# Deformable stage: ScalarE's queue issues seven of the fifteen position loads of a band

## The reference, cut to what matters

```python
offsets = conv2d(x, offset_w, offset_b)              # 18 channels: 9 taps, y and x
mod = jax.nn.sigmoid(conv2d(x, mod_w, mod_b))
sy = base_y[None, None, :, None] + off[:, 0]
sx = base_x[None, None, None, :] + off[:, 1]
...
sampled = (1.0 - wy1f) * ((1.0 - wx1f) * g00 + wx1f * g01) + wy1f * ((1.0 - wx1f) * g10 + wx1f * g11)
out = jnp.einsum('bckp,ock->bop', sampled, wk).reshape(B, O, Ho, Wo)
out = out * mod.mean(axis=1, keepdims=True) + bias[None, :, None, None]
```

## Time and profile before

| what | value |
|---|---|
| median of 3 runs | 3482.6 us (3479.66 to 3482.98) |
| the profiled execution, its time | 3484.76 us |
| its span, first to last instruction | 3483.1 us |
| mean granted TensorE clock | 0.861 of full |
| PE busy, share of the span | 2587.9 us, 74% |
| DVE busy | 2105.3 us, 60% |
| ACT busy | 1818.8 us, 52% |
| POOL busy | 1148.6 us, 33% |

### The profile page before, as it was taken

How to read it: one execution, slowest core, us unless ns; L and a number is a source line. 1 busy time by engine, 2 the same in 40 slices (tenths; PEclk the granted TensorE clock), 3 DMA queues, 4 the chain that set the end, 5 groups by cost and what they waited for, 6 DMA issues and landing times. The chain is left out here.

```text
span 3483.1 us, 86393 instructions
## 1 busy us (share of the span) xinstructions
PE 2587.9 (74%) x38569; PEld 1522.5 (44%) x38569; DVE 2105.3 (60%) x2867; ACT 1818.8 (52%) x1855; POOL 1148.6 (33%) x788
## 2 busy tenths in 40 slices
PE   1773838375999809599999927499993468999998
PEld 1763313124777603255555512277772124555554
DVE  5996766844555466366666566355554645666664
ACT  1211735663555538366656647355553655665565
POOL 0220000104555317444444310155541364334441
PEclk7886969687999959699999968699997787999999
DMA  2455030411111172122222250111115321222221
GB/s 59 129 152 155 1 97 16 177 18 26 33 26 31 37 279 42 47 73 75 75 70 73 70 207 7 27 27 27 30 30 195 122 52 59 72 72 73 72 71 54
DMA packets 213124, 257.74 MB, mean 74 GB/s; under 512 B 79188, under 2 KB 141192, under 8 KB 210696
## 3 DMA queue, kind: packets, MB, share of 16 engines
q1 hardware_dynamic: 203528, 218.58, 21.9%
q0 software_dynamic: 9216, 33.56, 2.4%
HBM read 153.52 MB, written 98.57 MB: 72 GB/s over the span
## 5 line engine op out<-in xcount | busy, mean ns | idle before, releaser
L2049 PE MATMUL dense_spread<-dense_cp,kept_spread_yx 32*128 32x512 f32 x2432 | 524.0, 707 | 137.2 <-DVE dense_hat L2220 67.3
L1320 ACT ACTIVATE snake_samp<-snake_s 128x1024 f32<-128x1024 f32 x320 | 321.0, 1023 | 299.8 <-PE snake_s L1250 299.6
L2220 DVE TENSOR_TENSOR dense_hat<-dense_spread,dense_hat 128x1024 f32<-128x1024 f32 x256 | 301.1, 1218 | 227.5 <-PE dense_spread L2049 227.3
L1383 DVE TENSOR_SCALAR snake_hat<-snake_spread 128x1024 f32<-128x1024 f32 x256 | 301.5, 1219 | 205.2 <-PE snake_spread L1228 205.2
L2151 ACT ACTIVATE dense_hat<-dense_spread 128x1024 f32<-128x1024 f32 x256 | 248.7, 1022 | 320.2 <-PE dense_spread L2049 316.3
L2097 PEld LDWEIGHTS dense_s<-dense_hat,dense_xt 64*64 64x64 f32 x11264 | 288.3, 141 | 154.3 <-issue 104.4
L1250 PE MATMUL snake_s<-snake_hat,snake_xt 64*64 64x128 f32 x10240 | 337.5, 274 | 19.3 <-ACT snake_samp L1320 19.0
L2171 ACT ACTIVATE dense_samp<-dense_s 128x864 f32<-128x864 f32 (+1 forms) x384 | 299.2, 833 | 93.6 <-PE dense_s L2097 93.5
L2097 PE MATMUL dense_s<-dense_hat,dense_xt 64*64 64x108 f32 x11264 | 332.3, 269 | 0.5
L1250 PEld LDWEIGHTS snake_s<-snake_hat,snake_xt 64*64 64x64 f32 x10240 | 285.0, 133 | 85.9 <-issue 42.2
L657 PE MATMUL dcnoff_acc<-dcnoff_low,kept_w_off 128*64 128x512 f32 x384 | 173.7, 607 | 198.9 <-DVE dcnoff_high L647 194.2
(11 more groups left out here) (315 smaller groups left out, 4878.6 us busy)
## 6 DMA issues: line engine op xcount, KB each, us to landing
dense_cp<-offs SPq DMA_DIRECT2D x576, 56.0 KB
x<-blur_x SPq DMA_DIRECT2D x16, 1024.0 KB, 5.1
gateconv_xn<-x SPq DMA_DIRECT2D x16, 1024.0 KB, 11.0
pre<-snake_ob SPq DMA_DIRECT2D x32, 512.0 KB, 3.9
dense_xr<-x SPq DMA_DIRECT2D x64, 256.0 KB, 3.2
out<-dense_xr SPq DMA_DIRECT2D x64, 256.0 KB, 2.5
dense_cp<-offs SPq DMA_DIRECT2D x256, 48.0 KB
offs<-dcnoff_cm SPq DMA_DIRECT2D x64, 144.0 KB
```

The source lines that it names most:

```text
L1320: act.activation(samp[u % 2][:, :, i * MS:(i + 1) * MS, :, :].rearrange("p b m t h -> p b (m t h)"), sample_at(u, i)[:, :, :], ACT.Copy).t ...
L1383: ins = dve.tensor_scalar(strided(hat[u % 2][:, 0:1], GUARD + (4 * tau + 2 * half) * SW * SR, [[8, 2], [SW * SR, 2], [SR, SW], [1, 8]]), s ...
L2049: return pe.matmul(bank[:, :], k.spread_yx[r, kind, :], cp[u % 2][r, tile, :], start=True, stop=True)
L2220: dve.tensor_tensor(h, p_hat[pair][:, :, :].rearrange("p t (r x) -> p (t r) x", x=W), h, ALU.mult).then_inc(main_ready, 1)
```

## The change

`put` moves out of SyncE's block and takes the queue as an argument. SyncE keeps the four y loads and the four x loads of tile 0. ScalarE issues the four x loads of tile 1, the two of tile 3 and the modulation: for bands 0 and 1 ahead of everything else, and for band u+2 at the head of iteration u, behind copy_samples(u-1, 5) and ahead of keep_y(u+1, 0). The bytes, the buffers and the semaphore count are as before.

```diff
+        def put(queue, u, tile, block_, ch, times):
+            at = offs[ch, 0, 4 * u, 0:1]
+            queue.dma_start(cp[u % 2][32 * block_:32 * block_ + GI * times, tile, :],
+                            bass.AP(tensor=at.tensor, offset=at.offset, ap=[[H * W, GI], [0, times], [1, 4 * W]])).then_inc(loaded[u % 2], 16)
+
         @block.sync
         def _(sp):
             def load(u):
-                def put(tile, block_, ch, times):
...
-                for tile in range(2):
-                    for i in range(4):
-                        put(tile, i, K2 + 2 * i + tile, 7)
-                put(3, 0, 2 * K2 - 1, 7)
-                put(3, 1, K2 - 1, 3)
-                sp.dma_start(cp[u % 2][64:64 + GI, 3, :], offs[MOD, :, 4 * u:4 * u + 4, :].rearrange("b h w -> b (h w)")).then_inc(loaded[u % 2], 16)
+                for i in range(4):
+                    put(sp, u, 0, i, K2 + 2 * i, 7)
...
+            def load(u):
+                for i in range(4):
+                    put(act, u, 1, i, K2 + 2 * i + 1, 7)
+                put(act, u, 3, 0, 2 * K2 - 1, 7)
+                put(act, u, 3, 1, K2 - 1, 3)
+                act.dma_start(cp[u % 2][64:64 + GI, 3, :], offs[MOD, :, 4 * u:4 * u + 4, :].rearrange("b h w -> b (h w)")).then_inc(loaded[u % 2], 16)
+
             act.wait_ge(cleared, 2)
+            act.wait_ge(ones_set, 1)
+            load(0)
+            load(1)
             keep_y(0, 0)
...
             for u in range(NB4):
                 more = u + 1 < NB4
+                if u + 2 < NB4:
+                    act.wait_ge(mod_spread, u + 1)
+                    load(u + 2)
                 if more:
                     keep_y(u + 1, 0)
```

More of the change, by code:

```diff
@@ L1970, in load @@
             def load(u):
-                def put(tile, block_, ch, times):
-                    at = offs[ch, 0, 4 * u, 0:1]
-                    sp.dma_start(cp[u % 2][32 * block_:32 * block_ + GI * times, tile, :],
-                                 bass.AP(tensor=at.tensor, offset=at.offset, ap=[[H * W, GI], [0, times], [1, 4 * W]])).then_inc(loaded[u % 2], 16)
                 for i in range(4):
```

## The result

| what | before | after |
|---|---|---|
| median | 3481.5 us (3479.66 to 3482.98, 4 runs) | 3628.6 us (3625.14 to 3628.97, 4 runs) |
| span of the profiled execution | 3483.1 us | 3627.1 us |
| mean granted TensorE clock | 0.861 | 0.855 |

The changed kernel is slower: ratio 1.0416, interval 1.0401 to 1.043. That is 147 us, where the forecast was 84.

A forecast was written before the change was run, and what follows sets the result against it. Position loads were taken to set the pace at least in part; afterwards the computing loop would. Interval 18.7 + 0.9 = 19.6 us against 18.08, times 60, minus 7 at starts: +84 us, 3567 us, range 3435 to 3670.

The forecast's parts named there:

- my own signs of being wrong: ScalarE's issue far from 0.65 us, or the 2.0 us TensorE gap lowering the clock in nearly every band or none.
- When ScalarE starts to issue: Head of the iteration: issues held behind copy_samples 4 and 5, starting 1.3 us after T0, when mod_spread lets SyncE begin.
- The rival in which the sequencer runs past pending copies: ScalarE issues from T0, 0 to 4.4 us, keep_y at 4.5, interval 17.4 us, 3435 us; chance 0.12.
- Who waits for that: Computing loop: keep_y ends 7.7, weigh 10.4, finish 13.45, clip 15.2 us; next T0 at 18.7, loop 2.2 us longer.
- The loads: Position loads all issued by 5.7 us, landed by about 9 to 10; clip's 57 us of waits in bands go away.
- term for the interval at full clock: Time from one band's T0 to the next without falls of TensorE's clock: 18.7 us.
- ScalarE's price: Seven issues ahead of keep_y take 4.4 us, priced from SyncE's rows for the same transfers, 0.65 us each for six.
- The clock: TensorE's new 2.0 us gap lowers its clock in one band of two, 1.8 us a fall: 0.9 us a band.
- The start of the stage: From first load to first clip, 12.54 us before, a gain of 3.5 us at each of two starts: 7 us.
- Issues cheap on ScalarE: Rival: ScalarE's issues take 0.39 us each, 2.7 in all; interval about 17.3 us, 3429 us; chance 0.10.
- The queues take turns: Rival: SyncE and ScalarE issue alternately, pairs at 1.3 us, keep_y at 9.7; about 3808 us, half contention 3690; chance 0.13.
- It evens out: Rival: issues of 0.5 us or a clock that hardly falls; interval 18.0 to 18.4, 3475 to 3505 us; chance 0.10.

The follow-up runs named there:

- my first experiment: The changed kernel with ScalarE's seven issues moved behind the first keep_y and keep_odd: 3517.6 us, ratio 1.0088 to the kernel before.
- the run with seven steps: Against the kernel with seven issues behind keep_odd (3517.6 us), each x load's source walked repetition outermost, seven of four rows, not four of seven: 3373.4 us, ratio 0.9692.

## Why the prediction was right in sign and short in size

The measured 3628.6 us lies inside the range that was given, 3435 to 3670, and 4 us above the 3505 to 3625 that had a chance of 0.55. (That pair is off by a slip: by the prediction's own sum, intervals of 18.5 to 20.5 give 3501 to 3621.) The change was forecast at 84 us and is 147, by the path that was forecast; and one of my own signs of being wrong came true: the gap brings the clock down in nearly every band.

**The mechanism, step by step.** *When ScalarE starts to issue:* taken at 1.3, measured 1.32 in the band shown. The rival in which the sequencer runs past pending copies is refuted twice: by this row, and by the kernel whose issues stand ahead of the copies, which start at 0.01. The band above shows the finer point too: the issue at 1910.88 ran while the copy of 1910.50 was executing and the next, of 1911.29, had not begun. In these rows the sequencer goes past a copy that is executing and one whose samples are ready (1910.80), and stands while a copy still waits for them. *Who waits for that:* keep_y, TensorE's gap, weigh, finish, clip, as listed. *The loads:* clip's wait for them in the bands is gone, as said. The kernel before with seven transfers more (3647.9 us) shows that the place of the issues is enough for the loss.

**The sizes.** The term for the interval at full clock was too small, 18.7 us against 20.0 (20.02 in the kernel with 9 filler matmuls, 19.95 in the band at 3007.65). By that band it divides as follows.
- *ScalarE's price*, "I take 4.4": from 3008.97 to 3013.98 the seven took 5.01, and keep_y starts at 6.43 instead of 5.8: +0.63. The value came from a queue that issued alone. With two that issue at once, issues are longer: 0.605 to a median of 0.743 on SyncE, and 3.64/5 = 0.73 on ScalarE.
- *spread_x ends 0.65 us behind keep_y's end:* it took 1.18 (3016.02 to 3017.20), so weigh ends at 11.49 instead of 10.4: +0.46 beside the first term. Its second four matmuls wait for keep_y's second copy, where before all eight ran in one go behind weigh.
- *finish and clip* from the end of weigh: 4.99 us against the 4.8 of the forecast, +0.19. Within it the parts changed places: clip took 3.32 us where I had 1.73, and the last instruction of finish 0.93 where it took 2.31.

These give 1.28 us; with 3.47 instead of 3.55 to the next T0 it is 19.95 against 18.7.

**The clock.** I had 1.8 us a fall in one band of two. It fell in nearly every band: the chain of waits in order of time names weigh's second part at 3.0 to 3.7 us in 26 of the second group's bands, these two among them.

```profile
3305.41 3.16 PE dense_s L2105 x32
3325.88 3.17 PE dense_s L2105 x32
```

But a fall cost only 0.6, by the kernel with 9 filler matmuls (0.5 by the ratios). Weigh ends 1.65 us later (13.14 against 11.49), and of this clip gives most back, as far as the two bands show: it takes 1.71 us in the low band and 3.32 in the full one. In the full band GpSimd's addition of rows (2.37 us from 3020.30) runs beside clip, in the low band it is over (1.92 us from 1922.23, clip from 1924.62). So the clock was worth 28 to 36 us instead of 54: I had too few falls and too high a price for one, two errors that partly cancelled. That is luck.

**The start of the stage.** Taken at 3.5 us each, measured 12.54 - 11.35 = 1.2 in the first and, from 2937.08 to 2947.84 where it took 12.25, 1.5 in the second.

**The sum by these numbers:** 84, plus 60 x 1.3 = 78 for the interval at full clock, minus 60 x 0.3 = 18 for the clock, plus 4 for the starts: 148, where 147 was measured. With 28 us for the clock it would be 140, so the close fit says little; the term for the interval at full clock is the large one either way.

**The rivals.** *Issues cheap on ScalarE:* refuted; the shortest x issue is 0.612 us. *The queues take turns:* right in kind and about a fifth of its size; an issue grows by 0.13, not by 0.6. The Trainium skill's lock on the descriptor generator ("Perfetto Trace Analysis", section "DMA Instruction — HWDGE (DVE, Sync)") agrees with the rows only if it is held for a small part of an issue. *It evens out:* refuted.

**What I had in hand and did not use.** The prediction worked out that few engines might carry the transfers, 6.5 us of them on four, and dropped it because they would still land before clip. That holds for the change itself, whose computing loop is longer. It is the step that failed in my first experiment: I took a load to land 2.7 us behind its last issue, and with issues spread over 8.6 us instead of 9.8 it took 4.4, in a band at full clock 5.2. What the loads wait for there is their own transfer and not the queue, as the run with seven steps shows; that the same held in the kernel before is argued from the 2.7 us, and from its DMA share of 0.23 over 7 us of issuing: 3.7 engines' worth, close to the 4.0 at which the loads of the changed kernel landed when nothing was being issued.

**What stays open.** Whether SyncE alone, as before, would do as well as 3373 with the repetition outermost was not tried; nor was a kernel that also permutes the constants by partition, so that it computes the reference's output with that order. Of kernels that compute it, three issues on ScalarE is the fastest here, 3420.6 us, and with the input rows first 3414.6, which is not to be told from it.

## What to carry to other kernels

- An issue on a computing engine's queue holds up all that stands behind it in that engine's order for its whole time; a copy already under way runs beside it. Seven of 0.65 to 0.73 us ahead of a copy on which TensorE waits cost 2.5 us a band; three set TensorE back by 0.6 us and gained more than that. Count how much slack the next instruction has, and move no more issues than fit in it.
- Before moving issues to another queue, ask whether the issue or the transfer is late. If the last load lands much later behind its issue when the issues come closer together, as it did here (2.7, then 4.4 to 5.2, at the start of a stage 5.7 us), suspect the transfer, and the shape of the access pattern is the thing to change.
- A gap that the change opens on TensorE should be priced twice, once for the wait and once for the clock behind it, and the second against what the later engines do beside it.

## What the runs showed of the hardware that I had not expected

- With two queues issuing at the same time, SyncE's x issue went from 0.605 to a median of 0.743 us and the input rows' from 0.352 to 0.662. With the seven issues behind keep_odd, where the two queues overlap less, the median is 0.615.
- The order of two dimensions in a load of 28 rows, same bytes and same number of transfers, changed a kernel's time from 3517.6 to 3373.4 us, though each issue became 0.12 us dearer; the DMA share while loads land at the stage start went from 0.25 to 0.41 of 16 engines.
- TensorE at the lower clock for 3.3 us of a band of 20 cost the band about 0.6 us where weigh alone was 1.65 late: VectorE's clip then no longer ran beside GpSimd's addition and took 1.71 us against 3.32. That the one is the cause of the other was not tried.
